# Second stage of a two-layer graph and state-space kernel: the convolution's running sum moved from SBUF to the projection's PSUM bank

## Chip, cores and metric

The kernel runs on one core of one Trainium2 chip. The metric is the device time of one execution in microseconds (us), taken as the median over several runs. The engines are TensorE (PE, matrix products; PEld is its weight load), VectorE (DVE), ScalarE (ACT), GpSimd (POOL) and SyncE (SP, which only issues transfers). Each engine works through its own list of instructions in order, and waits on semaphores for the others.

## What is computed

Two layers work on x (4096 rows of 256 numbers) and a 4096 x 4096 matrix adj. Layer 0 is a weighted neighbour sum and a Mamba-2 block, layer 1 a graph convolution with a selective scan, and a mixture of experts. The change lies in the selective scan of layer 1, whose reference is:

```python
h = jax.nn.relu(adj @ x @ gcn_w + gcn_b)
h = layer_norm(h) * ln_g + ln_b
xz = h @ w_in
xc, z = (xz[:, :D_INNER], xz[:, D_INNER:])            # D_INNER = 512
xpad = jnp.pad(xc, ((D_CONV - 1, 0), (0, 0)))         # D_CONV = 4
xconv = sum((xpad[k:k + L] * conv_w[:, k] for k in range(D_CONV))) + conv_b
u = jax.nn.silu(xconv)
dbc = u @ w_xp
dt = jax.nn.softplus(dbc[:, :DT_RANK] @ w_dt + b_dt)
B = dbc[:, DT_RANK:DT_RANK + D_STATE]                 # D_STATE = 16
C = dbc[:, DT_RANK + D_STATE:]
dA = jnp.exp(dt[:, :, None] * A[None])
dBu = dt[:, :, None] * B[:, None, :] * u[:, :, None]
def step(hst, inp):
    dAt, dBut, Ct = inp
    hst = dAt * hst + dBut
    return (hst, hst @ Ct)
_, ys = lax.scan(step, jnp.zeros((D_INNER, D_STATE), h.dtype), (dA, dBu, C))
y = ys + u * D_skip
y = y * jax.nn.silu(z)
return y @ w_out
```

## The kernel before

All data is float32. Positions are cut into 8 blocks of TB = 512, and features lie on the 128 partitions, so that D_INNER is four parts m = 0 to 3 of 128x512. The kernel has three stages. The first (to about 1110 us) is layer 0, the second (about 1110 to 2330 us) is the graph convolution and the selective scan of layer 1, the third is the mixture of experts.

In the second stage each block has 64 scan units: one for each of the 16 states n and the four parts m. A unit k is, on ACT, the exponential of dt times A into one of the PSUM banks ps4 and ps5; on POOL, the product dB of du and a broadcast row; on DVE, the recurrence itself (L1428, `scan`, h<-ps,hst,dB); and then four transposes on PE (L920) into one of the banks ps1, ps6 and ps7. The transposed result times a column of C is added to acc, on DVE (L1402), or on ACT (part) and POOL (L2199) for some (n, s), as the function `adder` says. DVE adds (`gather`) with a lag of 7 units behind its scans. The transposes of a unit on PE wait until the bank has been read, three transposes ago, and so PE cannot run more than about a unit ahead of DVE's sums, and DVE needs PE's transposes two units later.

Beside the scan of block ib run three other lists: `product_h`, PE's matmuls of adj for the blocks to come (L670, called p below); `post_b`, the output projection of the block before; and `pre_b` of the block after, which the change touches. `pre_b` normalises h (hb), then projects it part by part: b is the xc projection of part m (L856 and L858) into bank ps2, z the gate's projection (L861, L863) into bank ps3. A semaphore pair full and evac guards each bank: PE may write b of part m+1 only when b of part m has counted evac. ACT copies b to xcb (SBUF, with three columns of the block before ahead of it, the halo), and also writes tap 3 of the convolution, b times cw1 plus bias, to u (SBUF), which counts evac for the bank. DVE adds the other three taps, each one scalar_tensor_tensor (L1336) that reads xcb shifted by k and u and writes u. For each pair of parts ACT then takes tanh(u) and tanh(z's copy sz), and DVE finishes the two silu products (L1346). Last come the matmuls for dbc and dt, and the softplus of dt.

The order of the lists is fixed when the program is written. Each list is a generator that yields at slots; `beside` and `order_b` lay the 64 units of `scan` evenly over a block, the NPB slots of `pre_b` between 0.40 and 0.97 of it, and the 18 slots of `post_b` between 0.125 and 0.40. All engines follow the same list of slots, and a yield with nothing in it leaves a slot empty. `pre_load` says for each slot how much DVE work it is taken to hold; from it the table sets where PE's p matmuls go. Before the scan of block 0, `order_second` runs `pre_b(0)` beside 32 p steps alone, without POOL work; that stretch is called the opening below. So `pre_b` runs 8 times, once in the opening and 7 times beside a scan.

The lines of the prediction are: DVE L1322 and L1326 (subtraction of the mean, product with the root, hb<-hb,ps), L1336 (taps), L1346 (silu), L1355 (dt), L1402, L1428; PE L568 and L570 (mean square of the norm), L856 to L863, L670, L920; ACT L1615 (a helper, so its groups are told apart by tiles); POOL L2216 (dB) and L2199 (acc).

Of the kernel before, what the change touches and what calls it, by code (L numbers as in the profile page):

```python
# [9 lines left out]
ALU = mybir.AluOpType  # L10
ACT = mybir.ActivationFunctionType
# [111 lines left out]
def build(nc, t):  # L123
    with ExitStack() as ctx:
# [185 lines left out]

        NP, NPA, NSA, NPB, NPO = 64, 55, 62, 69, 18
        order_msg = [braid(("a", 9, 0, 1), ("b", 9, 0, 1), ("p", 16, 0, 1) if i else ("w", 4, 0.6, 1)) for i in range(NB // 2)]
# [23 lines left out]
        post_load = [1] * 8 + [0, 0] + mean_var  # L336
        pre_load = mean_var + [0, 0, 0] + ([1, 1, 0, 1, 1, 0] * 2 + [0] * 4) * 2 + [0, 2, 2, 0] + [1, 0, 1, 0, 0, 0, 0, 0, 0, 0] * 2 + [0, 0]
        beside = []
# [215 lines left out]
        def _(e):  # L554
# [291 lines left out]
            def pre_b(ib):  # L846
# [6 lines left out]
                for m in range(4):  # L853
                    b, z = preb_use(ib, 2 + 2 * m), preb_use(ib, 3 + 2 * m)
                    w.wait_ge(b.evac, b.n - 1)
                    e.matmul(b.ps[:, :], w1[:, 0, m * 128:(m + 1) * 128], hb[:, 0, :], start=True, stop=False)  # L856
                    yield
                    e.matmul(b.ps[:, :], w1[:, 1, m * 128:(m + 1) * 128], hb[:, 1, :], start=False, stop=True).then_inc(b.full, 1)  # L858
                    yield from (None, None)
                    w.wait_ge(z.evac, z.n - 1)  # L860
                    e.matmul(z.ps[:, :], w1[:, 0, 512 + m * 128:640 + m * 128], hb[:, 0, :], start=True, stop=False)  # L861
                    yield
                    e.matmul(z.ps[:, :], w1[:, 1, 512 + m * 128:640 + m * 128], hb[:, 1, :], start=False,  # L863
                             stop=True).then_inc(z.full, 1)
                    yield from (None, None)
                    if m % 2:
                        yield from (None, None, None, None)
                yield
# [196 lines left out]
        def _(e):  # L1065
# [251 lines left out]
            def pre_b(ib):  # L1317
# [11 lines left out]
                for m in range(4):  # L1329
                    b, c, at = preb_use(ib, 2 + 2 * m), u[p][:, m, :], 12 * ib + 3 * m  # L1330
                    yield from (None, None, None)
                    w.wait_ge(S("xcb"), 4 * ib + m + 1)
                    w.wait_ge(b.evac, b.n)
                    for k in range(3):
                        w.wait_ge(S("conv1"), at + k)
                        e.scalar_tensor_tensor(c, xcb[:, m, k:k + TB], col("cw1", 4 * m + k), c, ALU.mult,  # L1336
                                               ALU.add).then_inc(S("conv1"), 1)
                        yield
                    if m % 2:
                        for what in (u[p][:, m - 1:m + 1, :], sz[p][:, m - 1:m + 1, :]):  # L1340
# [262 lines left out]
        def _(e):  # L1603
# [229 lines left out]
            def pre_b(ib):  # L1833
# [8 lines left out]
                for m in range(4):  # L1842
# [7 lines left out]
                    act(xcb[:, m, 3:TB + 3], b.ps[:, :], ACT.Identity).then_inc(S("xcb"), 1)  # L1850
                    act(u[p][:, m, :], b.ps[:, :], ACT.Identity, scale=col("cw1", 4 * m + 3), bias=col("cb1", m)).then_inc(b.evac, 1)
                    yield from (None, None, None)
# [3 lines left out]
                    yield  # L1856
                    if m % 2:
                        yield
                        w.wait_ge(S("conv1"), 12 * ib + 3 * m + 3)
                        w.wait_ge(S("th1r"), n_th)  # L1860
# [6 lines left out]
                        yield  # L1867
                w.wait_ge(S("conv1"), 12 * ib + 12)
                act(xcb[:, :, 0:3], xcb[:, :, TB:TB + 3], ACT.Identity).then_inc(S("halo1"), 1)
# [422 lines left out]
```

## Time and profile before

| | us |
|---|---|
| median of 3 runs | 2549.93 (2549.86 to 2556.5) |
| the profiled execution's own time | 2553.42 |
| its span in the trace | 2551.6 |
| second stage's scans | about 1180 to 2320 |
| DVE busy over the span | 2021.9 |
| PE busy over the span | 2284.6 |

Busy time is an average over stages. Durations of neighbouring instructions in a row of the trace overlap a little: where two rows of DVE follow each other, the start of the second less the start of the first is what one costs. PE's trace shows each float32 matmul of `pre_b` and p as two records, and its rows join several; again the distance of starts counts (two records of 128x512 take 0.86 us, four of 128x256 take 0.86 us, four transposes of 128x128 0.44 us).

### The profile page before, as it was taken

The numbers are of one execution on the slowest core, as the hardware profiler recorded it, in microseconds if no ns is written. First come the engines' busy times: TensorE is split into PE (matmuls) and PEld (weight loads), VectorE is DVE, ScalarE is ACT, GpSimd is POOL, SyncE is SP. The second block draws the span as 40 slices with busy tenths as digits, with TensorE's granted clock in tenths as the row PEclk, the third lists the DMA queues.
The fourth block names the chain that finished last, engine by engine and source line by source line (L and its number), as shares of the span: only waits on it lengthen the run. The fifth ranks groups of instructions, "written<-read, shape, count | busy, mean of one in ns | idle before, by whom it ended". The sixth has DMA issues, their size and how long they took to land.

```text
span 2551.6 us, 26153 instructions
## 1 busy us (share of the span) xinstructions
PE 2284.6 (90%) x8964; PEld 1420.2 (56%) x8964; DVE 2021.9 (79%) x2224; ACT 1474.1 (58%) x2192; POOL 1198.9 (47%) x906
## 2 busy tenths in 40 slices
PE   7998999999999999988989888988998886675998
PEld 4444555545555545546666565665666563343886
DVE  5666878787877866325999999999999999997765
ACT  4676666576767553225655746565674656563444
POOL 2102231314141322305878778787887878793100
PEclk9999999999999999999989999899999998598999
DMA  5232222222222231133223232322323220112121
GB/s 214 90 98 91 66 91 87 86 75 83 88 83 86 74 124 40 51 101 124 92 83 116 75 123 76 106 92 83 116 81 118 75 91 33 42 50 79 62 67 49
DMA packets 111445, 221.15 MB, mean 87 GB/s; under 512 B 7586, under 2 KB 65186, under 8 KB 110930
## 3 DMA queue, kind: packets, MB, share of 16 engines
q1 hardware_dynamic: 107106, 204.00, 24.7%
q0 software_dynamic: 3664, 14.45, 1.5%
q8 instruction: 71, 1.16, 0.2%
q10 hardware_dynamic: 544, 1.05, 0.1%
q14 instruction: 60, 0.49, 0.1%
HBM read 199.28 MB, written 20.19 MB: 86 GB/s over the span
## 4 chain that ended last, share of the span: by engine, by line
PE 42%; DVE 24%; POOL 12%; issue 12%; ACT 9%; DMA 0%; DVEq 0%; POOLq 0%; ACTq 0%; SPq 0%
PE ps L628 9%; POOL dB L2216 7%; DVE h L1428 5%; PE ps L670 4%; DVE wgt L1106 4%; DVE wgt L1099 3%; PE ps L920 3%; DVE acc L1402 2%; PE ps L797 2%; ACT ps L1615 2%; POOL acc L2199 2%; ACT th L1615 2%; PE ps L652 2%; POOL du L2212 2%; PE ps L732 2%
## 5 line engine op out<-in xcount | busy, mean ns | idle before, releaser
L2216 POOL TENSOR_TENSOR dB<-du,bc 128x512 f32<-128x512 f32 x512 | 673.1, 1332 | 124.8 <-DVE h L1428 119.2
L1428 DVE TENSOR_TENSOR_SCAN h<-ps,hst,dB 128x512 f32<-128x512 f32 x512 | 643.4, 1271 | 48.4 <-ACT ps L1615 36.7
L628 PE MATMUL ps<-wgt,msg 128*128 128x512 f32 x1024 | 498.1, 595 | 15.1 <-DVE wgt L1106 13.6
L1615 ACT ACTIVATE ps<-dt,cols 128x512 f32<-128x512 f32 x512 | 350.9, 687 | 272.4 <-DVE h L1428 268.8
L920 PE MATMUL ps<-consts,h 128*128 128x128 f32 x2048 | 342.9, 295 | 152.3 <-DVE acc L1402 91.2
L670 PE MATMUL ps<-raw,msg 128*128 128x256 f32 x1792 | 468.9, 397 | 0.9 <-ACT hb L1615 0.9
L920 PEld LDWEIGHTS ps<-consts,h 128*128 128x128 f32 x2048 | 258.6, 150 | 335.4 <-DVE acc L1402 153.6
L670 PEld LDWEIGHTS ps<-raw,msg 128*128 128x128 f32 x1792 | 337.2, 200 | 85.8 <-issue 49.9
L628 PEld LDWEIGHTS ps<-wgt,msg 128*128 128x128 f32 x1024 | 186.6, 190 | 219.4 <-issue 191.7
L1615 ACT ACTIVATE wgt<-wgt 128x1024 f32<-128x1024 f32 x256 | 258.4, 1049 | 56.2 <-DVE wgt L1099 54.6
L2199 POOL TENSOR_TENSOR acc<-acc,part 128x512 f32<-128x512 f32 x160 | 219.4, 1371 | 87.8 <-ACT part L1615 84.1
L1402 DVE SCALAR_TENSOR_TENSOR acc<-ps,Ct,acc 128x512 f32<-128x512 f32 x305 | 220.8, 724 | 3.7 <-PE ps L920 3.6
L1099 DVE SCALAR_TENSOR_TENSOR wgt<-wgt 128x1024 f32<-128x1024 f32 x128 | 176.8, 1421 | 47.7 <-ACT wgt L1615 47.7
L1106 DVE SCALAR_TENSOR_TENSOR wgt<-raw,wgt 128x1024 f32<-128x1024 f32 x128 | 171.2, 1378 | 5.0 <-ACT wgt L1615 4.8
L1336 DVE SCALAR_TENSOR_TENSOR u<-xcb,cols,u 128x512 f32<-128x512 f32 x96 | 119.7, 1247 | 13.0 <-ACT u L1615 11.8
L1613 ACT ACT_TABLE_LOAD x78 | 100.1, 1283 | 51.5 <-DVE cc L1177 23.2
L1615 ACT ACTIVATE wgt<-raw 128x1024 f32<-128x1024 f32 x128 | 128.0, 1047 | 0.8 <-DMA raw<-in_adjT 0.6
L2142 POOL DMA_DIRECT2D tmp_x<-xb x8 | 5.5, 691 | 258.0 <-DVE xb L1260 258.0
L2111 POOL TENSOR_TENSOR E<-E,cbm 128x1024 f32<-128x1024 f32 x32 | 76.7, 2397 | 92.6 <-ACT E L1615 66.8
L1177 DVE SCALAR_TENSOR_TENSOR cc<-xbc,cols,cc 128x512 f32<-128x512 f32 x120 | 110.1, 918 | 2.9
L1615 ACT ACTIVATE part<-ps,Ct 128x512 f32<-128x512 f32 x160 | 107.3, 671 | 4.9 <-PE ps L920 4.9
L2106 POOL TENSOR_TENSOR xdec<-xdt,ecd 128x512 f32<-128x512 f32 x32 | 33.4, 1045 | 146.0 <-DVE xdt L1212 146.0
(321 smaller groups left out, 3563.4 us busy)
## 6 DMA issues: line engine op xcount, KB each, us to landing
raw<-in_adjT SPq DMA_DIRECT2D x256, 512.0 KB, 3.6
bc<-tmp_bc SPq DMA_DIRECT2D x64, 512.0 KB, 4.9
xb<-in_xT POOLq DMA_DIRECT2D x8, 512.0 KB, 4.1
tmp_x<-xb POOLq DMA_DIRECT2D x8, 512.0 KB, 3.1
x<-tmp_x SPq DMA_DIRECT2D x8, 512.0 KB, 5.4
tmp_x<-x SPq DMA_DIRECT2D x8, 512.0 KB, 4.1
raw<-tmp_xn SPq DMA_DIRECT2D x8, 512.0 KB, 4.1
tmp_xn<-x SPq DMA_DIRECT2D x7, 512.0 KB, 3.6
```

The source lines that it names most:

```text
L628: x = e.matmul(P[d][:, :], msg[:, j, d * 128:(d + 1) * 128], wgt[g % NW][:, l, :], start=j == 0, stop=j == NJ - 1)
L670: x = e.matmul(P[0][:, 256 * d:256 * d + 256], msg[:, j, d * 128:(d + 1) * 128], quarters(g)[:, l, :], start=j == 0 and d == 0, stop=j == ...
L920: i = e.transpose(b.ps[:, m * 128:(m + 1) * 128], hr[n % 3][:, m, s * 128:(s + 1) * 128], ident)
L1099: e.scalar_tensor_tensor(wgt[i % NW][:, :, :], wgt[i % NW][:, :, :], -2.0, wgt[i % NW][:, :, :], ALU.add, ALU.mult).then_inc(S("q"), 1)
L1106: e.scalar_tensor_tensor(wgt[i % NW][:, :, :], raw[i % 4][:, :, :], 1.0, wgt[i % NW][:, :, :], ALU.is_lt, ALU.mult).then_inc(S("wgt"), 1)
L1177: e.scalar_tensor_tensor(c, xbc[:, m, k:k + TB], col("cw0", 4 * m + k), c, ALU.mult, ALU.add).then_inc(S("conv"), 1)
L1336: e.scalar_tensor_tensor(c, xcb[:, m, k:k + TB], col("cw1", 4 * m + k), c, ALU.mult, ALU.add).then_inc(S("conv1"), 1)
L1402: e.scalar_tensor_tensor(acc[:, s, :], b.ps[:, :], c, acc[:, s, :], ALU.mult, ALU.add).then_inc(b.evac, 1)
L1428: e.tensor_tensor_scan(hr[n % 3][:, m, :], PS[4 + k % 2].t[:, :], dBr[k % 4][:, :], hst[:, n % 16, m:m + 1], ALU.mult, ALU.add).then_inc(S ...
L1615: return e.activation(out, in_, func, bias=bias, scale=scale)
L2199: e.tensor_tensor(acc[:, s, :], acc[:, s, :], part[HANDED[j] % 2][:, :], ALU.add).then_inc(S("summed"), 1)
L2216: e.tensor_tensor(dBr[k % 4][:, :], du[:, m, :], bcr[i % 3][:, n % 2, :], ALU.mult).then_inc(S("dB"), 1)
```

## The change

Tap 3 no longer goes to u. ACT writes it back into the projection's own bank ps2, in place, and signals a new semaphore `tap` (it first waits for its own copy to xcb). DVE's taps 0 and 1 read xcb and ps2 and write ps2; tap 2 reads xcb and ps2 and writes u in SBUF, and only it counts evac of the bank. So u is no longer an input of a tap, and the bank is held from the projection to the end of the third tap. The two tanh of ACT wait for evac where they waited for `conv1`, and `conv1` counts two taps a part where it counted three. To space the side work for this, the even parts get two more empty slots on PE, ACT and DVE, NPB goes from 69 to 73 and `pre_load` gets the zeros for them.

```diff
-        NP, NPA, NSA, NPB, NPO = 64, 55, 62, 69, 18
+        NP, NPA, NSA, NPB, NPO = 64, 55, 62, 73, 18
...
-        pre_load = mean_var + [0, 0, 0] + ([1, 1, 0, 1, 1, 0] * 2 + [0] * 4) * 2 + [0, 2, 2, 0] + [1, 0, 1, 0, 0, 0, 0, 0, 0, 0] * 2 + [0, 0]
+        pre_load = mean_var + [0, 0, 0] + ([1, 1, 0, 1, 1, 0] + [0] * 2 + [1, 1, 0, 1, 1, 0] + [0] * 4) * 2 + [0, 2, 2, 0] + [1, 0, 1, 0, 0, 0, 0, 0, 0, 0] * 2 + [0, 0]
...
# PE, pre_b, behind z of part m
-                    if m % 2:
-                        yield from (None, None, None, None)
+                    yield from [None] * (4 if m % 2 else 2)
...
# DVE, pre_b
-                    b, c, at = preb_use(ib, 2 + 2 * m), u[p][:, m, :], 12 * ib + 3 * m
+                    b, at = preb_use(ib, 2 + 2 * m), 8 * ib + 2 * m
                     yield from (None, None, None)
                     w.wait_ge(S("xcb"), 4 * ib + m + 1)
-                    w.wait_ge(b.evac, b.n)
+                    w.wait_ge(S("tap"), 4 * ib + m + 1)
                     for k in range(3):
                         w.wait_ge(S("conv1"), at + k)
-                        e.scalar_tensor_tensor(c, xcb[:, m, k:k + TB], col("cw1", 4 * m + k), c, ALU.mult,
-                                               ALU.add).then_inc(S("conv1"), 1)
+                        out, signal = (b.ps[:, :], S("conv1")) if k < 2 else (u[p][:, m, :], b.evac)
+                        e.scalar_tensor_tensor(out, xcb[:, m, k:k + TB], col("cw1", 4 * m + k), b.ps[:, :], ALU.mult,
+                                               ALU.add).then_inc(signal, 1)
                         yield
...
# ACT, pre_b
                     act(xcb[:, m, 3:TB + 3], b.ps[:, :], ACT.Identity).then_inc(S("xcb"), 1)
-                    act(u[p][:, m, :], b.ps[:, :], ACT.Identity, scale=col("cw1", 4 * m + 3), bias=col("cb1", m)).then_inc(b.evac, 1)
+                    w.wait_ge(S("xcb"), 4 * ib + m + 1)
+                    act(b.ps[:, :], b.ps[:, :], ACT.Identity, scale=col("cw1", 4 * m + 3), bias=col("cb1", m)).then_inc(S("tap"), 1)
...
-                        w.wait_ge(S("conv1"), 12 * ib + 3 * m + 3)
+                        for x in (preb_use(ib, 2 * m), b):
+                            w.wait_ge(x.evac, x.n)
```

In the following lists of instructions a row is a line, an operation and its tiles (with buffer numbers, h0 to h2 the scan's output, raw0 to raw3 adj), and the semaphores it waits for; the recurrence is printed under the name SCALAR_TENSOR_TENSOR too. Lines shift by a few behind the edit: L919 is L920 before, L1337 L1336, L1405 L1402 and L1431 L1428.

DVE, beside the scan of block 1, from the first tap of part 0 to the first tap of part 1; before:

```order
L1428 SCALAR_TENSOR_TENSOR h0<-ps5,hst,dB1 128x512 [waits dB,exp]
L1402 SCALAR_TENSOR_TENSOR acc<-ps6,Ct1,acc 128x512 [waits evac1,full6]
L1336 SCALAR_TENSOR_TENSOR u0<-xcb,cols,u0 128x512 [waits conv1,evac2,xcb]
L1336 SCALAR_TENSOR_TENSOR u0<-xcb,cols,u0 128x512 [waits conv1]
L1428 SCALAR_TENSOR_TENSOR h0<-ps4,hst,dB2 128x512 [waits dB,exp]
L1402 SCALAR_TENSOR_TENSOR acc<-ps7,Ct1,acc 128x512 [waits evac6,full7]
L1336 SCALAR_TENSOR_TENSOR u0<-xcb,cols,u0 128x512 [waits conv1]
L1428 SCALAR_TENSOR_TENSOR h0<-ps5,hst,dB3 128x512 [waits dB,exp]
L1428 SCALAR_TENSOR_TENSOR h1<-ps4,hst,dB0 128x512 [waits hst,dB,exp]
L1336 SCALAR_TENSOR_TENSOR u0<-xcb,cols,u0 128x512 [waits conv1,evac2,xcb]
```

and now:

```order
L1431 SCALAR_TENSOR_TENSOR h2<-ps5,hst,dB3 128x512 [waits dB,exp]
L1431 SCALAR_TENSOR_TENSOR h0<-ps4,hst,dB0 128x512 [waits hst,dB,exp]
L1337 SCALAR_TENSOR_TENSOR ps2<-xcb,cols,ps2 128x512 [waits tap,xcb]
L1431 SCALAR_TENSOR_TENSOR h0<-ps5,hst,dB1 128x512 [waits dB,exp]
L1405 SCALAR_TENSOR_TENSOR acc<-ps6,Ct1,acc 128x512 [waits evac1,full6]
L1337 SCALAR_TENSOR_TENSOR ps2<-xcb,cols,ps2 128x512 [waits conv1]
L1337 SCALAR_TENSOR_TENSOR u0<-xcb,cols,ps2 128x512 [waits conv1]
L1431 SCALAR_TENSOR_TENSOR h0<-ps4,hst,dB2 128x512 [waits dB,exp]
L1405 SCALAR_TENSOR_TENSOR acc<-ps7,Ct1,acc 128x512 [waits evac6,full7]
L1431 SCALAR_TENSOR_TENSOR h0<-ps5,hst,dB3 128x512 [waits dB,exp]
L1431 SCALAR_TENSOR_TENSOR h1<-ps4,hst,dB0 128x512 [waits hst,dB,exp]
L1337 SCALAR_TENSOR_TENSOR ps2<-xcb,cols,ps2 128x512 [waits tap,xcb]
```

The first tap stands one scan and one sum earlier, and three scans and one sum lie between the last tap of part 0 and the first of part 1, where two scans lay.

PE at the same place, from z of part 0 (the last rows into ps3) to the projection of part 1 into ps2; before:

```order
L861 MATMUL ps3<-hb,w1 128x512 [waits evac3]
L920 MATMUL ps1<-consts,h2 128x128 [waits scan,evac1]
L920 MATMUL ps1<-consts,h2 128x128 x3
L863 MATMUL ps3<-hb,w1 128x512
L670 MATMUL ps0<-raw2,msg 128x256 x2
L920 MATMUL ps6<-consts,h2 128x128 [waits evac6]
L920 MATMUL ps6<-consts,h2 128x128 x3
L856 MATMUL ps2<-hb,w1 128x512 [waits evac2]
L858 MATMUL ps2<-hb,w1 128x512
L920 MATMUL ps7<-consts,h2 128x128 [waits evac7]
```

and now:

```order
L863 MATMUL ps3<-hb,w1 128x512
L919 MATMUL ps1<-consts,h2 128x128 [waits scan,evac1]
L919 MATMUL ps1<-consts,h2 128x128 x3
L670 MATMUL ps0<-raw2,msg 128x256 [waits d_raw2]
L670 MATMUL ps0<-raw2,msg 128x256 x3
L919 MATMUL ps6<-consts,h2 128x128 [waits evac6]
L919 MATMUL ps6<-consts,h2 128x128 x3
L670 MATMUL ps0<-raw2,msg 128x256 x2
L856 MATMUL ps2<-hb,w1 128x512 [waits evac2]
L919 MATMUL ps7<-consts,h2 128x128 [waits evac7]
L919 MATMUL ps7<-consts,h2 128x128 x3
L858 MATMUL ps2<-hb,w1 128x512
```

Between z of part 0 and the first matmul of part 1 lay two p and one set of four transposes; now six p and two sets lie there, and a third set lies between the two matmuls of part 1.

PE at the norm of the same block (L568 and L570 read sq1 and fill ps3); before:

```order
L920 MATMUL ps1<-consts,h0 128x128 [waits evac1]
L920 MATMUL ps1<-consts,h0 128x128 x3
L568 MATMUL ps3<-sq1,consts 128x512 [waits evac3,sq1]
L920 MATMUL ps6<-consts,h0 128x128 [waits evac6]
L920 MATMUL ps6<-consts,h0 128x128 x3
L670 MATMUL ps0<-raw0,msg 128x256 x2
L570 MATMUL ps3<-sq1,consts 128x512
L920 MATMUL ps7<-consts,h1 128x128 [waits scan,evac7]
```

and now:

```order
L919 MATMUL ps1<-consts,h0 128x128 [waits evac1]
L919 MATMUL ps1<-consts,h0 128x128 x3
L568 MATMUL ps3<-sq1,consts 128x512 [waits evac3,sq1]
L570 MATMUL ps3<-sq1,consts 128x512
L919 MATMUL ps6<-consts,h0 128x128 [waits evac6]
L919 MATMUL ps6<-consts,h0 128x128 x3
L670 MATMUL ps0<-raw0,msg 128x256 x2
```

The two matmuls now stand together, without a set of transposes and a row of p between them. On DVE the product with the root (L1326 before) stands one scan and one sum closer behind the subtraction.

## Rows read from the trace of the kernel before

**Rows 1.** Page part 1: engine, busy us (share of span), instructions.

```profile
PE 2284.6 (90%) x8964; PEld 1420.2 (56%) x8964; DVE 2021.9 (79%) x2224; ACT 1474.1 (58%) x2192; POOL 1198.9 (47%) x906
```

**Rows 2.** Busy us by stretch: PE, PEld, DVE, ACT, POOL; PE clock, DMA, GB/s.

```profile
1320.00:1460.00 140.00, 124.47 (x570) 86.89 (x567) 130.06 (x129) 83.99 (x137) 108.90 (x83) 0.95 0.29 96
1390.00:1418.00 28.00, 24.28 (x109) 15.93 (x108) 27.32 (x26) 18.05 (x29) 24.26 (x17) 1.00 0.19 61
```

**Rows 3.** DVE groups, 1180 to 2320: busy us, mean ns | idle before, releaser.

```profile
L1428 DVE TENSOR_TENSOR_SCAN h<-ps,hst,dB 128x512 f32<-128x512 f32 x512 | 643.4, 1271 | 48.4 <-ACT ps L1615 36.7 <-POOL dB L2216 11.6
L1402 DVE SCALAR_TENSOR_TENSOR acc<-ps,Ct,acc 128x512 f32<-128x512 f32 x301 | 217.9, 724 | 1.2 <-PE ps L920 1.2
L1336 DVE SCALAR_TENSOR_TENSOR u<-xcb,cols,u 128x512 f32<-128x512 f32 x84 | 110.7, 1318 | 1.0
```

**Rows 4.** DVE waits, 1180 to 2320: who, for whom, us, times, longest.

```profile
DVE hb L1326 <- ACT ps L1615: 8.4, 7, 1.5
```

**Rows 5.** The taps in the opening, DVE groups 1100 to 1180.

```profile
L1336 DVE SCALAR_TENSOR_TENSOR u<-xcb,cols,u 128x512 f32<-128x512 f32 x12 | 9.0, 752 | 12.0 <-ACT u L1615 11.8
```

**Rows 6.** DVE in time: start us, us, instruction, count; taps of block 1.

```profile
1390.40 3.04 DVE L1336 SCALAR_TENSOR_TENSOR u<-xcb,cols,u 128x512 f32<-128x512 f32 x2
1393.37 1.27 DVE L1428 TENSOR_TENSOR_SCAN h<-ps,hst,dB 128x512 f32<-128x512 f32 x1
1394.56 0.72 DVE L1402 SCALAR_TENSOR_TENSOR acc<-ps,Ct,acc 128x512 f32<-128x512 f32 x1
1395.20 1.33 DVE L1336 SCALAR_TENSOR_TENSOR u<-xcb,cols,u 128x512 f32<-128x512 f32 x1
```

**Rows 7.** POOL in the same stretch, in time.

```profile
1391.16 4.82 POOL L2216 TENSOR_TENSOR dB<-du,bc 128x512 f32<-128x512 f32 x3
...
1397.81 1.27 POOL L2216 TENSOR_TENSOR dB<-du,bc 128x512 f32<-128x512 f32 x1
```

**Rows 8.** ACT groups, 1180 to 2320.

```profile
L1615 ACT ACTIVATE u<-ps,cols 128x512 f32<-128x512 f32 x28 | 21.7, 775 | 0.0
...
L1615 ACT ACTIVATE sz<-ps 128x512 f32<-128x512 f32 x28 | 16.6, 593 | 9.3 <-PE ps L863 9.3
...
L1615 ACT ACTIVATE ps<-ps 128x512 f32<-128x512 f32 x28 | 16.4, 587 | 9.7 <-PE ps L570 9.3
```

**Rows 9.** PE in time, norm and first projection of block 1.

```profile
1377.99 1.12 PE L568 MATMUL ps<-sq,consts 128*128 128x512 f32 x2
...
1380.54 1.02 PE L570 MATMUL ps<-sq,consts 128*128 128x512 f32 x2
...
1386.43 1.02 PE L856 MATMUL ps<-hb,w 128*128 128x512 f32 x2
1387.29 1.02 PE L858 MATMUL ps<-hb,w 128*128 128x512 f32 x2
1388.15 0.60 PE L920 MATMUL ps<-consts,h 128*128 128x128 f32 x4
1388.58 1.03 PE L670 MATMUL ps<-raw,msg 128*128 128x256 f32 x4
1389.45 1.02 PE L861 MATMUL ps<-hb,w 128*128 128x512 f32 x2
```

**Rows 10.** DVE in time, the product with the root.

```profile
1382.82 1.22 DVE L1326 TENSOR_TENSOR hb<-hb,ps 128x1024 f32<-128x1024 f32 x1 [1.15 <-ACT ps L1615]
```

**Rows 11.** ACT in time, opening: copy of part 2, tanh behind part 3.

```profile
1146.74 0.58 ACT L1615 ACTIVATE xcb<-ps 128x512 f32<-128x512 f32 x1
...
1155.00 1.06 ACT L1615 ACTIVATE th<-u 128x1024 f32<-128x1024 f32 x1 [0.54 <-DVE u L1336]
```

**Rows 12.** PE in time, opening: parts 2 and 3, silu-fed matmuls.

```profile
1144.20 1.02 PE L858 MATMUL ps<-hb,w 128*128 128x512 f32 x2
...
1149.37 1.02 PE L856 MATMUL ps<-hb,w 128*128 128x512 f32 x2
```

**Rows 13.** PE waits, 1180 to 2320, longest in total.

```profile
PE ps L920 <- DVE acc L1402: 91.2, 77, 3.9
```

More of the change, by code:

```diff
@@ L1329, in pre_b @@
                 for m in range(4):
-                    b, c, at = preb_use(ib, 2 + 2 * m), u[p][:, m, :], 12 * ib + 3 * m
+                    b, at = preb_use(ib, 2 + 2 * m), 8 * ib + 2 * m
                     yield from (None, None, None)
                     w.wait_ge(S("xcb"), 4 * ib + m + 1)
-                    w.wait_ge(b.evac, b.n)
+                    w.wait_ge(S("tap"), 4 * ib + m + 1)
                     for k in range(3):
                         w.wait_ge(S("conv1"), at + k)
-                        e.scalar_tensor_tensor(c, xcb[:, m, k:k + TB], col("cw1", 4 * m + k), c, ALU.mult,
-                                               ALU.add).then_inc(S("conv1"), 1)
+                        out, signal = (b.ps[:, :], S("conv1")) if k < 2 else (u[p][:, m, :], b.evac)
+                        e.scalar_tensor_tensor(out, xcb[:, m, k:k + TB], col("cw1", 4 * m + k), b.ps[:, :], ALU.mult,
+                                               ALU.add).then_inc(signal, 1)
                         yield
-                    if m % 2:
+                    if m % 2 == 0:
+                        yield from [None] * 2
+                    else:
                         for what in (u[p][:, m - 1:m + 1, :], sz[p][:, m - 1:m + 1, :]):
@@ L1856, in pre_b @@
                     yield
-                    if m % 2:
+                    if m % 2 == 0:
+                        yield from [None] * 2
+                    else:
                         yield
-                        w.wait_ge(S("conv1"), 12 * ib + 3 * m + 3)
+                        for x in (preb_use(ib, 2 * m), b):
+                            w.wait_ge(x.evac, x.n)
                         w.wait_ge(S("th1r"), n_th)
@@ L1867, in pre_b @@
                         yield
-                w.wait_ge(S("conv1"), 12 * ib + 12)
                 act(xcb[:, :, 0:3], xcb[:, :, TB:TB + 3], ACT.Identity).then_inc(S("halo1"), 1)
```

## Prediction

> **What bounds the kernel now.** I read the busy time of each engine first [rows 1], then the same by stretch [rows 2], then the groups and waits of DVE in the scans [rows 3, 4], then single instructions in time. PE has the largest share of the whole span (90%), but its share says little here, because PE's waits in the second stage are for DVE's sums: 91.2 us in 77 waits of the transposes [rows 13]. In a block of the scans (1320 to 1460) DVE is busy 130.06 us of 140, PE 124.47 and POOL 108.90; in the stretch with the taps (1390 to 1418) DVE is busy 27.32 us of 28, PE 24.28 [rows 2]. DVE waits 48.4 us for ACT and POOL before its scans in 1140 us, and before its taps 1.0 us [rows 3]. So DVE sets the pace, in the tap stretches all the more, and a microsecond that its taps lose is a microsecond of the kernel until PE or a chain takes over.
>
> What a tap costs depends on who is beside it. In the opening, with POOL idle, it takes 752 ns [rows 5]; beside the scan 1318 ns over 84 taps [rows 3]. A sum L1402 has the same size and reads one operand from PSUM, and takes 724 ns in the same stretch, 301 times over [rows 3]. The rows in time say why: two taps take 3.04 us from 1390.40 [rows 6], and POOL's three products from 1391.16 take 4.82 us, 1.6 each, where one that no tap meets takes 1.27 [rows 7]. They take turns: a tap waits for POOL's instruction in progress, and POOL's next waits for the tap. That is the price of reading both operands from SBUF.
>
> The Trainium skill ("SBUF — State Buffer", Who interferes with whom) says that a DVE instruction with two SBUF inputs contends with a GpSimd instruction that reads SBUF, and one with at most one SBUF input does not. The trace agrees, 1318 against 724 ns.
>
> **The change, part by part.** *Taps beside the scan.* Each now reads xcb from SBUF and the other operand from PSUM. I take the 724 ns of L1402: 84 x (1.318 - 0.724) = 49.9 us less DVE work. For the third tap (28 of the 84), which writes SBUF, L1402 is the same form. The first two write PSUM, and no DVE row does. The nearest are ACT's: in place in PSUM 587 ns, from PSUM to SBUF 593 [rows 8], so a PSUM output costs ACT nothing. Bounds for these 56 taps: below, the same 1% cheaper, 717 ns, which gives 0.4 us more; above, the 1.271 us of the scan [rows 3], the slowest DVE row of this size, which gives 56 x (1.271 - 0.724) = 30.6 us less gain. I take 724 ns, the nearest row in form.
> A rule speaks against the change: by the Trainium skill ("Perfetto Trace Analysis", Optimizing Scalar/DVE Operations) a DVE access costs about 60 ns on SBUF and 125 on PSUM. By it, as an estimate, the 84 taps would lose 65 ns each, 5.5 us in all. L1402 with a PSUM operand is not above the quiet 752 ns, so the trace does not show it.
>
> *Taps in the opening.* 12 x (752 - 724) ns, 0.3 us, nothing.
>
> *ACT.* The write to u (775 ns) becomes one to ps2 [rows 8], at the same price. New is the wait for its own copy to xcb: at present the second starts 0.49 us after the first though the first lasts 0.6; I put 0.15 us on each of 28, 4 us of ACT in all. ACT is busy 84 us of 140 [rows 2], so it counts only in the chains below.
>
> *POOL.* It gets back what the taps made it wait, some 0.3 us for each product that met one. DVE waited for dB only 11.6 us in all [rows 3], so I count nothing.
>
> *The longer hold.* This is the price. Before, PE could project part m+1 as soon as ACT had read part m. Now it waits for the last tap. The slots place the first matmul of part m+1 about one scan unit behind that tap on PE's list, and PE is tied to DVE by the transposes anyway. By starts, a scan costs 1.19 us and a sum 0.64 [rows 6], a projection matmul 0.86, four transposes 0.43 and two p 0.87 [rows 9]. For parts 0 to 1, counted from the end of the last tap: PE's first matmul to 0.95; the transposes behind it wait for DVE's next sum, at 1.83, to 2.27; the second matmul to 3.1; ACT's copy and write back 0.5 + 0.15 + 0.7 with 0.1 us for each signal, to about 4.65. DVE meanwhile has three scans and one sum, 3 x 1.19 + 0.64 = 4.2 us, and so waits 0.45 us. Parts 2 to 3 have the same distance: 0.45 us. Parts 1 to 2 have the silu products between and wait for nothing.
> The first tap of part 0 also has less room, as PE's two matmuls now have two p and a set of transposes between them. Before, the two stood together from 1386.43 to 1388.15 [rows 9], and the tap came at 1390.40 without a wait [rows 6]: 2.25 us, of which ACT's two writes need 1.4, so 0.85 were to spare. The chain is now longer by 0.87 + 0.43 on PE and 0.15 on ACT, 1.45 us: 0.6 us of it is not covered.
> In the norm the root's product stands one scan and one sum closer (1.83 us), where DVE waited 1.15 us already in this block [rows 10] and 8.4 us in seven [rows 4]. But L570 now follows L568 at once instead of 2.55 us later (1377.99 and 1380.54, [rows 9]), so that the root comes 1.7 us sooner. Net 0.3 us.
> Before the tanh of the second pair DVE has one scan less cover: 0.2 us. Together 0.45 + 0.45 + 0.6 + 0.3 + 0.2 = 2.0 us a block, 14 us in seven blocks.
>
> *The opening.* Part 2 is projected by 1144.20 + 0.86 = 1145.06 [rows 12], ACT's copy comes at 1146.74 [rows 11], so the three taps end at about 1150.5. PE has five pieces of 0.86 us (p, z) before part 3 and is there at 1149.4: it waits 1.1 us. A further p pair stands between part 3's matmuls, 0.9 us. The tanh at 1155.00 [rows 11] comes 2 us later, and the start of the scans with it: +2 us.
>
> **Sum.** -49.9 + 14 + 2 = -34 us. Of the profiled execution's 2553.4 us that leaves 2519.5; the median of the three runs is 3.5 us lower, so I predict 2516.
>
> **The rivals.**
> *A, the full gain.* The waits are covered after all, since a wait at one tap fills the queues and spares the next wait (DVE's 36.7 us for ACT [rows 3] may shrink too): 2550 - 50 = 2500. For it: the table gives one unit of distance; against: three scans and a sum are just the length of the chain.
> *B, PE becomes the bound in the tap stretch.* PE has 16 projection matmuls (13.8 us), about 32 p (13.8) and 17 sets of transposes (7.3) in the 17 units from the first projection to the last: 34.9 us. DVE there needs 36 us after the change and 43 before. If PE needs idle time at the share of now (24.28 busy of 28, [rows 2]), the stretch takes 40.2 us, and a block gains 3 us instead of 5: 7 x 3 - 2 = 19 us, 2530.
> *C, PSUM outputs are slow on DVE.* At 1.271 us for 56 taps: -49.9 + 30.6 + 16 = -3, so 2547, no change that can be told.
> *D, slower: the handover between parts falls out of step.* PE waits for the last tap with scan transposes queued behind it; DVE's next sum waits for those, and only after it come DVE's next scans and taps. Then the chain of two matmuls and two ACT writes, 3.3 us, is not covered but added. With 3 handovers in each of 7 blocks it costs 69 us, and 2550 - 50 + 69 + 2 = 2571. It decides against the change once a handover costs DVE more than 50/21 = 2.4 us, that is, lasts over 6.6 us where 4.2 are covered. Against it: in DVE's list the taps come behind the sum for which PE's transposes wait, and PE reaches the wait about a unit after the tap.
> *E, the taps are bound by something else than POOL* (the kernel does not do what it says, 1318 ns stay): 2550 + 16 = 2566. The 752 ns of the opening [rows 5] speak against it.
>
> **How the numbers follow.** Forecast 0.45, A 0.19, B 0.18, C 0.09, D 0.05, E 0.04. The range from 2498 to 2538 holds the forecast, A and B with some PSUM cost on each. A measurement of this kernel tells about 0.3% (8 us) from no change. Faster by more: forecast, A and B, and a little of C, 0.84. Within: most of C, 0.09. Slower: D, E and rest, 0.07.
>
> **What would show it.** The taps' groups: about 724 ns for both outputs, POOL's products near 1270 ns. DVE's idle before the first taps of parts 1 and 3 of some 0.4 us each, released by ACT, where it was nothing; before the root's product a little over 1.15 us. PE's waits at L856 for the tap short, under 0.5 us beside the scan, about 1 us once in the opening. DVE's busy time falls by 50 us; the span falls by less, and the difference stands as idle before taps. I am wrong if the taps that write PSUM read over 0.85 us, if DVE's scans and sums begin to wait for PE by more than 10 us in all (B), or if the first taps wait over 2 us each (D).

## The result

The changed kernel takes 2512.04 us (median of 4 runs, 2511.06 to 2513.26), against 2553.12 us (4 runs, 2549.86 to 2556.5) for the kernel before on the same chip. The ratio is 0.9839, with a 95% interval of 0.9821 to 0.9858, so it is 41 us (1.6%) faster. The forecast was 2516 us. The span of the profiled execution fell from 2551.6 to 2509.5 us, by 42.1 us.

The groups of DVE in the scans of the changed kernel answer to [rows 3] (busy us, mean ns | idle before, releaser):

```profile
L1431 DVE TENSOR_TENSOR_SCAN h<-ps,hst,dB 128x512 f32<-128x512 f32 x512 | 643.1, 1271 | 39.0 <-ACT ps L1618 27.4 <-POOL dB L2222 11.6
L1405 DVE SCALAR_TENSOR_TENSOR acc<-ps,Ct,acc 128x512 f32<-128x512 f32 x301 | 218.1, 725 | 1.8 <-PE ps L919 1.7
L1337 DVE SCALAR_TENSOR_TENSOR ps<-xcb,cols,ps 128x512 f32<-128x512 f32 x56 | 41.9, 748 | 19.1 <-ACT ps L1618 19.1
...
L1349 DVE SCALAR_TENSOR_TENSOR sz<-th,sz 128x1024 f32<-128x1024 f32 x14 | 21.6, 1539 | 0.0
L1337 DVE SCALAR_TENSOR_TENSOR u<-xcb,cols,ps 128x512 f32<-128x512 f32 x28 | 20.9, 748 | 1.0
...
L1349 DVE SCALAR_TENSOR_TENSOR u<-th,u 128x1024 f32<-128x1024 f32 x14 | 17.2, 1225 | 4.4 <-ACT th L1618 4.4
L1358 DVE SCALAR_TENSOR_TENSOR dt<-dt,th 128x1024 f32<-128x1024 f32 x14 | 16.9, 1207 | 0.0
...
L1325 DVE TENSOR_TENSOR hb<-hb,ps 128x1024 f32<-128x1024 f32 x7 | 8.5, 1221 | 11.3 <-ACT ps L1618 11.3
```

The taps take 748 ns in both forms, where they took 1318, and the form that writes PSUM costs what the form that writes SBUF does. The 84 taps now need 41.9 + 20.9 = 62.8 us instead of 110.7. But DVE now waits 20.1 us before them, where it waited 1.0. Two groups of the kernel before belong beside the others:

```profile
L1346 DVE SCALAR_TENSOR_TENSOR u<-th,u 128x1024 f32<-128x1024 f32 x14 | 22.6, 1613 | 4.0 <-ACT th L1615 4.0
...
L1346 DVE SCALAR_TENSOR_TENSOR sz<-th,sz 128x1024 f32<-128x1024 f32 x14 | 17.9, 1280 | 0.0
L1355 DVE SCALAR_TENSOR_TENSOR dt<-dt,th 128x1024 f32<-128x1024 f32 x14 | 17.5, 1250 | 4.0 <-ACT th L1615 4.0
```

DVE's time between the first scan and the last, by group (busy and idle before it):

| us | before | after | difference |
|---|---|---|---|
| taps, busy | 110.7 | 62.8 | -47.9 |
| taps, wait | 1.0 | 20.1 | +19.1 |
| root's product, wait | 8.4 | 11.3 | +2.9 |
| scans, wait for ACT | 36.7 | 27.4 | -9.3 |
| dt, wait and busy | 21.5 | 16.9 | -4.6 |
| silu, wait and busy | 44.5 | 43.2 | -1.3 |
| sum | | | -41.1 |

The first scan starts at 1181.14 us instead of 1180.08, the last at 2277.7 instead of 2317.5, so the scans shrank by 40.9 us. Behind the last scan 231.8 us are left where 234.1 were. That is TensorE's clock: the work is the same and the waits of PE behind the scans are alike, but the granted clock of the first 50 us there (a mean of its two levels, 1.2 and 2.4 GHz, as a share of the upper) was 0.80 before and 0.86 after. The same two pairs of matmul records there took 2.08 and 1.65 us before, and 1.12 and 1.02 after. Whether the change has a part in the clock is not shown. Both rows are of the view by stretches: from and to, length, the busy time of PE, PEld, DVE, ACT and POOL with their counts, then PE's granted clock, the DMA share and GB/s. The kernel before:

```profile
2330.00:2380.00 50.00, 32.67 (x109) 21.66 (x108) 34.70 (x63) 17.02 (x28) 4.11 (x2) 0.80 0.34 120
```

The changed kernel, in the same place of the program:

```profile
2289.00:2339.00 50.00, 32.68 (x117) 21.90 (x116) 36.11 (x66) 17.36 (x28) 4.15 (x2) 0.86 0.36 127
```

POOL in the tap stretch of block 1, in time, shows what answers to [rows 7]: no product takes over 1.28 us.

```profile
1385.63 1.28 POOL L2205 TENSOR_TENSOR acc<-acc,part 128x512 f32<-128x512 f32 x1 [1.35 <-ACT part L1618]
1386.86 2.50 POOL L2222 TENSOR_TENSOR dB<-du,bc 128x512 f32<-128x512 f32 x2
...
1391.07 1.27 POOL L2205 TENSOR_TENSOR acc<-acc,part 128x512 f32<-128x512 f32 x1
```

DVE at the handover from part 0 to part 1 of block 1 in the changed kernel, in time (start, length, instruction, idle before it and its releaser):

```profile
1387.72 0.75 DVE L1337 SCALAR_TENSOR_TENSOR u<-xcb,cols,ps 128x512 f32<-128x512 f32 x1
...
1393.40 0.76 DVE L1337 SCALAR_TENSOR_TENSOR ps<-xcb,cols,ps 128x512 f32<-128x512 f32 x1 [0.73 <-ACT ps L1618]
```

PE in the same place of the changed kernel, in time:

```profile
1389.13 1.02 PE L856 MATMUL ps<-hb,w 128*128 128x512 f32 x2
1390.36 0.66 PE L919 MATMUL ps<-consts,h 128*128 128x128 f32 x4 [0.21 <-DVE acc L1405]
1390.86 1.02 PE L858 MATMUL ps<-hb,w 128*128 128x512 f32 x2
```

The last tap of part 0 ends at 1388.39, and PE comes to the projection of part 1 (L856) at 1389.13 by its own list, not held by the bank. Then a set of transposes waits 0.21 us for DVE's sum, and only at 1390.86 does the second matmul (L858) start. ACT's copy and write follow, and DVE has waited 0.73 us when the next tap starts at 1393.40.

### The profile page after: what moved, and what is told of

Its sections match the earlier page's. It is cut to its first block, busy times and chain, and to the rows that moved or that the text cites. A ratio compares the mean times of both kernels' runs of the same rounds, so it can differ in the third digit from the quotient of the medians.

```text
span 2509.5 us, 26161 instructions
## 1 busy us (share of the span) xinstructions
PE 2276.5 (91%) x8964; PEld 1413.7 (56%) x8964; DVE 1971.0 (79%) x2224; ACT 1475.5 (59%) x2192; POOL 1186.5 (47%) x906
## 3 DMA queue, kind: packets, MB, share of 16 engines
q8 instruction: 71, 1.16, 0.2%
q10 hardware_dynamic: 544, 1.05, 0.1%
## 4 chain that ended last, share of the span: by engine, by line
PE 41%; DVE 24%; issue 13%; POOL 12%; ACT 9%; DMA 1%; DVEq 0%; SPq 0%; POOLq 0%; ACTq 0%
PE ps L628 9%; POOL dB L2222 8%; DVE h L1431 5%; DVE wgt L1105 4%; PE ps L670 3%; DVE wgt L1098 3%; PE ps L919 2%; DVE acc L1405 2%; PE ps L797 2%; POOL acc L2205 2%; ACT th L1618 2%; ACT ps L1618 2%; PE ps L903 2%; PE ps L652 2%; PE ps L732 2%
## 5 line engine op out<-in xcount | busy, mean ns | idle before, releaser
L2222 POOL TENSOR_TENSOR dB<-du,bc 128x512 f32<-128x512 f32 x512 | 663.7, 1314 | 102.6 <-DVE h L1431 98.4
L1431 DVE TENSOR_TENSOR_SCAN h<-ps,hst,dB 128x512 f32<-128x512 f32 x512 | 643.1, 1271 | 39.0 <-ACT ps L1618 27.4
L670 PE MATMUL ps<-raw,msg 128*128 128x256 f32 x1792 | 456.8, 392 | 0.9 <-ACT hb L1618 0.9
L919 PE MATMUL ps<-consts,h 128*128 128x128 f32 x2048 | 339.0, 292 | 114.6 <-DVE acc L1405 58.2
L919 PEld LDWEIGHTS ps<-consts,h 128*128 128x128 f32 x2048 | 254.8, 149 | 296.6 <-DVE acc L1405 126.9
L1405 DVE SCALAR_TENSOR_TENSOR acc<-ps,Ct,acc 128x512 f32<-128x512 f32 x305 | 221.0, 725 | 4.2 <-PE ps L919 4.0
L1618 ACT ACTIVATE g<-ps,b 128x512 f32<-128x512 f32 x64 | 43.2, 687 | 81.9 <-PE ps L1002 74.3
```

What stands on the lines that cost most here:

```text
L670: x = e.matmul(P[0][:, 256 * d:256 * d + 256], msg[:, j, d * 128:(d + 1) * 128], quarters(g)[:, l, :], start=j == 0 and d == 0, stop=j == ...
L919: i = e.transpose(b.ps[:, m * 128:(m + 1) * 128], hr[n % 3][:, m, s * 128:(s + 1) * 128], ident)
L1405: e.scalar_tensor_tensor(acc[:, s, :], b.ps[:, :], c, acc[:, s, :], ALU.mult, ALU.add).then_inc(b.evac, 1)
L1431: e.tensor_tensor_scan(hr[n % 3][:, m, :], PS[4 + k % 2].t[:, :], dBr[k % 4][:, :], hst[:, n % 16, m:m + 1], ALU.mult, ALU.add).then_inc(S ...
L1618: return e.activation(out, in_, func, bias=bias, scale=scale)
L2222: e.tensor_tensor(dBr[k % 4][:, :], du[:, m, :], bcr[i % 3][:, n % 2, :], ALU.mult).then_inc(S("dB"), 1)
```

## The experiments

### Which part of the change does it: the spacing or the sum in PSUM

**Spacing alone.** The kernel before with 73 slots and the empty slots, the sum in SBUF:

```diff
-        NP, NPA, NSA, NPB, NPO = 64, 55, 62, 69, 18
+        NP, NPA, NSA, NPB, NPO = 64, 55, 62, 73, 18
...
-                    if m % 2:
-                        yield from (None, None, None, None)
+                    yield from [None] * (4 if m % 2 else 2)
```

(with the zeros in `pre_load`, and two empty slots behind the even parts on DVE and ACT too).

> The kernel before with only the spacing of the change: 73 slots, two empty slots behind the even parts on PE, ACT and DVE, the running sum in SBUF as before. Theory (the gain is the taps' own time): taps stay at about 1318 ns beside the scan, 2553 us within 8 us; a few us less are possible if the shorter waits of the scans for ACT (27.4 us after, 36.7 before) come from the spacing. Rival (the spacing brings the gain, by spreading PE's and DVE's side work): 2530 us or less.

Measured: 2561.44 us against 2555.13, ratio 1.0025 (1.0016 to 1.0035), a loss of 6 us. DVE's groups there:

```profile
L1429 DVE TENSOR_TENSOR_SCAN h<-ps,hst,dB 128x512 f32<-128x512 f32 x474 | 596.5, 1272 | 40.3 <-ACT ps L1616 28.7 <-POOL dB L2219 11.6
...
L1335 DVE SCALAR_TENSOR_TENSOR u<-xcb,cols,u 128x512 f32<-128x512 f32 x84 | 117.9, 1404 | 14.5 <-ACT xcb L1616 10.6 <-issue 3.0
...
L1356 DVE SCALAR_TENSOR_TENSOR dt<-dt,th 128x1024 f32<-128x1024 f32 x14 | 16.9, 1208 | 0.0
```

The taps are slower still, 1404 ns, and DVE waits 14.5 us before them, though no bank is held. The scans' wait for ACT is down to 28.7 us and dt's wait is gone: these two savings of the changed kernel come from the spacing. They do not pay for the waits and the slower taps. (The view ends at 2270, 38 scans short; the waits of the scans are the same to the last scan.)

**The sum in PSUM without the spacing.** The changed kernel with 69 slots and without the empty slots:

```diff
-        NP, NPA, NSA, NPB, NPO = 64, 55, 62, 73, 18
+        NP, NPA, NSA, NPB, NPO = 64, 55, 62, 69, 18
...
-                    yield from [None] * (4 if m % 2 else 2)
+                    if m % 2:
+                        yield from (None, None, None, None)
```

> The changed kernel with the old 69 slots and no empty slots behind the even parts: the sum in PSUM alone. Theory (the hold is paid in the handover from the last tap to the next part's first): taps stay at 748 ns, but the first taps of parts 1 and 3 have two scans to cover the chain where they have three and a sum; 1.8 us more wait at 14 places, about 25 us, 2530 to 2540 us. Rival (the hold is harmless, PE comes late enough anyway): 2505 to 2516 us.

Measured: 2546.65 us, ratio 0.9965 (0.9951 to 0.998). It is 8 us faster than the kernel before and 35 us slower than the changed one, somewhat above the range expected. Who waited for whom there, with the total in us, the number of times and the longest; first DVE:

```profile
DVE ps L1338 <- ACT ps L1617: 38.6, 14, 5.4
```

And PE of the same kernel:

```profile
PE ps L856 <- DVE u L1338: 33.3, 14, 3.1
```

PE stands at the bank for 33.3 us at 14 places, and DVE waits 38.6 us for ACT before the taps. This is the price of the hold when nothing is placed for it. The sum in PSUM and the spacing are worth little each alone, -8 and +6 us, and -41 together.

### Whose wait is it: the bank's, or that of two matmuls that stand apart

In the changed kernel a set of transposes stands between the two projection matmuls of a part, in parts 0 and 3 with a row of p as well; in part 1 of block 1 that set waits for DVE (the 0.21 us above). The next edit removes the slot between them:

```diff
                     e.matmul(b.ps[:, :], w1[:, 0, m * 128:(m + 1) * 128], hb[:, 0, :], start=True, stop=False)
-                    yield
                     e.matmul(b.ps[:, :], w1[:, 1, m * 128:(m + 1) * 128], hb[:, 1, :], start=False, stop=True).then_inc(b.full, 1)
-                    yield from (None, None)
+                    yield from (None, None, None)
```

**In the changed kernel.**

> The changed kernel with the two projection matmuls of each part in one slot of PE's list, so that no transposes or p stand between them; number of slots as in the changed kernel. Theory (DVE's 19.1 us before the first taps are the chain from the last tap through PE's set of transposes, which waits for DVE's sum): the second matmul ends at 1.8 us instead of 3.1 us behind the last tap, the waits of parts 1 and 3 vanish and part 0's falls from 1.05 to about 0.2 us; 10 to 17 us less, 2495 to 2503 us. Rival (those waits stand for a PE that is the bound in the tap stretch): the waits move to DVE's sums or scans, 2508 to 2514 us.

Measured: 2495.55 us, ratio 0.9767 (0.975 to 0.9783), 16.5 us less than the changed kernel. DVE's waits between the scans in this kernel:

```profile
DVE h L1430 <- ACT ps L1617: 28.2, 30, 2.1
...
DVE ps L1336 <- ACT ps L1617: 4.1, 9, 1.2
```

DVE's wait for ACT before the taps fell from 19.1 us in 21 places to 4.1 in 9. Its wait for PE's transposes before the sums stayed (1.7 us to the last scan in both kernels), and so did the scans' for ACT (28.2 us, 27.4 in the changed kernel).

**With the sum in SBUF and the spacing.**

> The kernel before with the spacing and with the two projection matmuls of each part together; the sum in SBUF. Theory (standing together only shortens the chain behind the hold): the same as spacing alone, 2561 us within 6. Rival (it speeds PE or ACT up in general, the 16.5 us it gave the changed kernel have nothing to do with the hold): 2545 us.

Measured: 2543.84 us, ratio 0.9957 (0.994 to 0.9973). The theory failed: the same edit gains 17.6 us over spacing alone (2561.44), where no bank is held until the last tap. DVE's wait before the taps fell from 14.5 to 2.8 us:

```profile
L1334 DVE SCALAR_TENSOR_TENSOR u<-xcb,cols,u 128x512 f32<-128x512 f32 x84 | 120.7, 1437 | 2.8 <-ACT xcb L1615 1.8
```

So most of the wait that I had put down to the hold is the chain from PE's first matmul to the tap, stretched by the transposes between the two matmuls. The spacing shifted the slots so that this happens for part 0 and part 1, too.

**In the kernel before.**

> The kernel before with only the two projection matmuls of each part together. Theory (their standing apart costs only where DVE's taps come up against the chain from the projection, and in the kernel before they wait 1.0 us in all): no change, 2548 to 2558 us. Rival (it is a gain of about 17 us in any layout, as it was behind the spacing with either form of the sum): 2538 us.

Measured: 2554.62 us against 2554.36, ratio 1.0 (0.9991 to 1.001). Where DVE does not wait before its taps, the edit is worth nothing. The theory held here: the edit gains 16 to 18 us with the spacing in either form of the sum, where DVE waits before its taps, and nothing here.

**With the sum in PSUM and no spacing.**

> The sum in PSUM with the old 69 slots (no spacing), and the two projection matmuls of each part together. In the sum-in-PSUM run without spacing DVE waited 39.1 us before its taps, at 14 places, two of them in each block, and PE 33.3 us at the projection for the last tap; in that layout parts 0 and 1 had their matmuls together already, parts 2 and 3 apart. Theory (without spacing the hold itself is the wait: PE stands at the bank right behind the last tap's slot): only the parts with matmuls apart gain, about 7 x 2 us, 2528 to 2536 us, and PE's wait at the projection stays near 33 us. Rival (also there the waits come from the matmuls standing apart): the waits fall below 10 us and the time to 2505 us or less.

Measured: 2530.94 us, ratio 0.9904 (0.9887 to 0.992), 16 us less than without the edit. So the gain needs no spacing either, only a wait of DVE before its taps. That wait fell from 38.6 to 27.4 us: before part 3, whose matmuls stood apart, from 4.1 or 4.2 us to between 2.1 and 3.0 in the five middle blocks, while before part 1, whose matmuls stood together already, 1.19 us stayed. PE's wait at the bank in this kernel:

```profile
PE ps L856 <- DVE u L1337: 32.4, 14, 3.3
```

PE's wait at the bank stayed (32.4 us), as expected. So without the spacing the hold costs, and the spacing takes that away (5.9 us with it, in the changed kernel with the matmuls together).

The medians beside each other, in us (they come from several chips, on which the kernel before has medians of 2553 to 2556, so that a difference between two of them is good to about 3 us):

| | sum in SBUF | sum in PSUM |
|---|---|---|
| old slots, matmuls as they were | 2555 | 2546.65 |
| old slots, together | 2554.62 | 2530.94 |
| spacing, matmuls as they were | 2561.44 | 2512.04 |
| spacing, together | 2543.84 | 2495.55 |

With the spacing, the sum in PSUM is worth 49 us in one row and 48 in the other. Without it 8 and 24.

### Why a tap with two SBUF inputs is slow

**POOL reads nothing.** Both products of POOL become fills with zeros:

```diff
-                e.tensor_tensor(acc[:, s, :], acc[:, s, :], part[HANDED[j] % 2][:, :], ALU.add).then_inc(S("summed"), 1)
+                e.memset(acc[:, s, :], 0.0).then_inc(S("summed"), 1)
...
-                e.tensor_tensor(dBr[k % 4][:, :], du[:, m, :], bcr[i % 3][:, n % 2, :], ALU.mult).then_inc(S("dB"), 1)
+                e.memset(dBr[k % 4][:, :], 0.0).then_inc(S("dB"), 1)
```

> The kernel before with POOL's two scan products replaced by a fill with zeros of the same tiles (no product du x bc, no sum acc + part: this part of the computation is left out), so that POOL reads no SBUF there. Theory (a tap waits because POOL reads SBUF): the taps L1336 beside the scan take about 750 ns as in the opening, min to max within 0.1 us. Rival (they wait for something else in the scans, such as transfers or ACT's writes): 1300 ns.

Measured, in one run: 2481.97 us. The taps beside the scan:

```profile
L1336 DVE SCALAR_TENSOR_TENSOR u<-xcb,cols,u 128x512 f32<-128x512 f32 x84 | 62.4, 743 | 2.4 <-ACT xcb L1615 1.4
```

84 taps in the SBUF form take 743 ns (724 to 753 over all 96), with POOL still writing 665 tiles of the same size in that stretch. The fills do meet taps: in block 1 two of them, at 1384.50 and 1384.96, lie within two taps that together took 1.51 us from 1383.88. So a tap waits for POOL's reading of SBUF, and not for its writing, for transfers or for ACT, which went on as before. The time of this kernel says less, because POOL itself became faster (526 ns a fill, where a product took 1332), and part of the work is gone.

**One tap of each form.** ACT writes tap 3 to u; the three taps of DVE are then

```diff
-                        out, signal = (b.ps[:, :], S("conv1")) if k < 2 else (u[p][:, m, :], b.evac)
+                        part_, bank = u[p][:, m, :], b.ps[:, :]
+                        out, old, signal = ((bank, part_, S("conv1")), (part_, bank, S("conv1")), (part_, part_, b.evac))[k]
```

> The changed kernel and its spacing, but with ACT's tap 3 in SBUF (u), tap 0 from xcb and u (both SBUF) to PSUM, tap 1 from xcb and PSUM to u, tap 2 from xcb and u to u. Theory (two SBUF inputs make a tap wait for POOL, where it writes does not matter): the first and third form 1300 ns, the second 748 ns; 56 slow taps at 0.57 us more are 32 us, 2540 to 2548 us. Rival (the SBUF output is what meets POOL): the first form 750 ns, the other two 1300 ns, the same time. Rival (reading PSUM alone is enough to be fast only if the output is PSUM too): the second form is slow.

Measured: 2520.88 us, ratio 0.9862 (0.9846 to 0.9879). The three groups of taps in this kernel:

```profile
L1338 DVE SCALAR_TENSOR_TENSOR ps<-xcb,cols,u 128x512 f32<-128x512 f32 x28 | 24.1, 861 | 20.2 <-ACT u L1619 20.2
L1338 DVE SCALAR_TENSOR_TENSOR u<-xcb,cols,u 128x512 f32<-128x512 f32 x28 | 23.7, 846 | 1.0
...
L1338 DVE SCALAR_TENSOR_TENSOR u<-xcb,cols,ps 128x512 f32<-128x512 f32 x28 | 20.6, 735 | 0.0
```

The order of the forms is that of the theory: both forms with two SBUF inputs meet POOL, whether they write PSUM (861 ns) or SBUF (846), and the one with a PSUM input does not (735). The size is not: they lose about 0.11 us each and not 0.57, and the kernel lost 9 us and not 32. Part by part, the first tap took 0.76 us in the 14 places behind a scan, and behind a sum 0.77 in 7 places and 1.16 in 7; in the kernel before, two taps back to back took 1.2 to 1.5 us each on average (a row of 3.04 us for two, [rows 6]), and the second of such a pair 1.64 or 1.65 wherever the trace shows it by itself. My reading is that a tap loses what is left of POOL's product when it comes, and that a second one right behind it finds the next product ahead of it; the rows fit this, but no run tests it alone.

**The sum ahead of the scan.** In the kernel before, DVE's sum of each unit moved ahead of its scan, so that no tap stands behind a sum:

```diff
+                    j = k - LAG
+                    if j > 0 and j % 64 == 0:
+                        gates(j // 64 - 1)
+                    if j >= 0:
+                        gather(j)
                     if k < 64 * NB:
...
-                    j = k - LAG
-                    if j > 0 and j % 64 == 0:
-                        gates(j // 64 - 1)
-                    if j >= 0:
-                        gather(j)
                     yield
```

> The kernel before with DVE's sum of each unit ahead of its scan instead of behind it, so that every tap stands behind a scan or another tap, and none behind a sum. In the one-tap-of-each-form run, taps with two SBUF inputs took 0.76 us behind a scan and 0.77 to 1.16 behind a sum, and the changed kernel's gain would then depend on POOL's phase. Theory (a tap waits only for what is left of POOL's product, and POOL starts one when a scan ends): single taps 0.76 to 0.85 us, the second of a pair 1.2 to 1.6, the mean 1.0 to 1.1 us, so 20 us less than before if the sums are hidden as before, 2525 to 2540 us. Rival (every tap meets POOL at a random point): the mean stays at 1.3 us and the time at 2550 or above.

Measured: 2546.34 us, ratio 0.9982 with an interval of 0.996 to 1.0003, so a gain is not shown. Five of the six runs lie between 2544.66 and 2547.03, below all nine of the kernel before (2550.1 to 2555.89), and the sixth took 2561.19 at a mean granted clock of 0.946, where the others had 0.961 to 0.963. A gain of some 9 us is likely, then, and it is well short of the 2525 to 2540 us expected. DVE's groups in the scans of this kernel:

```profile
L1336 DVE SCALAR_TENSOR_TENSOR u<-xcb,cols,u 128x512 f32<-128x512 f32 x84 | 99.7, 1187 | 1.0
...
L1346 DVE SCALAR_TENSOR_TENSOR sz<-th,sz 128x1024 f32<-128x1024 f32 x14 | 25.1, 1791 | 0.0
...
L1355 DVE SCALAR_TENSOR_TENSOR dt<-dt,th 128x1024 f32<-128x1024 f32 x14 | 21.6, 1543 | 8.5 <-ACT th L1615 8.5
```

The taps' mean fell to 1187 ns, 11 us less in all, half of what I expected: single taps behind a scan took 0.72 to 0.79 us in 14 places, but 1.12 to 1.14 in the other 14. The other instructions with two SBUF inputs came to stand worse: the silu product sz<-th,sz went to 1791 ns from 1280, dt to 1543 from 1250. The place beside POOL matters, but moving one thing moves all, and which phase decides stays open. What does not stay open is that an input from PSUM removes the meeting in every place: in the kernel with one tap of each form all 28 taps of that form took 0.73 or 0.74 us, and the 84 of the changed kernel took 0.74 to 0.76.

### A faster version

**Matmuls together, and the root's product one slot later.** On DVE in `pre_b`, six empty slots ahead of the product with the root and four behind it, where five and five stood.

> The changed kernel with the two matmuls together, and on DVE the norm's product with the root one slot later (behind one scan and one sum more), the number of slots unchanged. It waits 1.6 us a block for the root now. Theory: that wait goes (11.3 us), but the chain from there to part 0's first tap has one scan and a sum less cover, about 1.0 us of 1.6 comes back there: 0 to 5 us less than with the matmuls together, 2490 to 2496 us. Rival (that wait was all cover for others): 2496 to 2500 us.

Measured: 2491.16 us (2490.67 to 2492.59), ratio 0.9754 (0.9738 to 0.977), the fastest of the kernels that compute everything. DVE's waits between the scans in this kernel:

```profile
DVE h L1430 <- ACT ps L1617: 30.8, 39, 2.1
DVE ps L1336 <- ACT ps L1617: 6.7, 14, 0.6
```

The wait for the root falls from 11.3 to 1.1 us; the taps wait 6.7 us instead of 4.1, and the scans for ACT 30.8 instead of 28.2 and for POOL 10.7 instead of 11.6, from the first scan to the last. The gain of 4.4 us over the kernel with the matmuls together lies in the range expected. The times of the two kernels do not overlap (2494.67 to 2497.42 there), but they are from two chips and the intervals of their ratios do overlap, so the gain is likely and not shown.

## Why the prediction was right, and where it was not

**The taps.** 49.9 us forecast, 47.9 measured. The price of 724 ns was 24 ns low: the taps take 748, close to their 752 in the quiet opening ([rows 5]), so that this row would have been the better choice. What the 24 ns are is open; a DVE instruction with a scalar from cols and one input in PSUM (L1411 before) takes 734. The open bound, the write to PSUM, costs nothing (rival C falls). The reason, POOL's reading, is shown by the fill experiment; rival E falls. The Trainium skill ("SBUF — State Buffer", Who interferes with whom) draws the same line, at a GpSimd instruction that reads SBUF and not at one that only writes it, and the 743 ns beside the fills agree. Its charge of 125 ns for an access to PSUM against 60 to SBUF ("Perfetto Trace Analysis", Optimizing Scalar/DVE Operations) is not seen: 748 ns for either output, and 752 with SBUF alone.

**ACT and POOL.** ACT's write to ps2 takes 751 ns (775 before) and starts 0.63 us behind the copy instead of 0.49, as forecast (0.15 us). POOL's gain brought nothing, as forecast: DVE waited 11.6 us for it before and after.

**The longer hold.** Here a step failed. I forecast 1.5 us a block of waits before taps (0.6, 0.45 and 0.45), and 2.7 came on average (1.05, 0.73 and 0.68 in block 1). The places and the releaser were right, and the transposes between the matmuls were in my chain, but I called the sum of it the price of the hold. The runs say otherwise. With the sum in SBUF the spacing alone makes DVE wait 14.5 us; with the matmuls together 5.1 us are left in the changed kernel, and 2.8 in SBUF. By these differences the hold itself costs 2 to 6 us of DVE's waits with the spacing, and the rest is the spacing's own doing. The hold shows at one handover: PE waits 0.79 us for the last tap before it projects part 3, once in each block, where I had put under 0.5 us. The slots that were put in for the longer hold moved the two matmuls of parts 0 and 1 apart.

**Norm, silu, opening.** The root's product waits 2.9 us more in seven blocks (2.1 forecast), the silu 0.4 (1.4). The 2.1 did not follow from its own terms: 1.83 us less cover and a root 1.7 us sooner leave 0.1 us a block and not 0.3, and 0.4 came. The opening costs 1.06 us and not 2: PE's wait for the last tap of part 2 was 1.26 us (1.1 forecast), but the norm's two matmuls together, which I counted in the blocks, help in the opening too, where the root's product starts at 1125.20 instead of 1126.64.

**What was missing.** The sum ended at -34 us and -42.1 came. The difference is what I did not look for: more room between the pieces of `pre_b` also shortens waits. The scans wait 9.3 us less for ACT and dt 4.0 us less, which the spacing alone shows as well (28.7 us and none). That makes up for the waits before the taps, 19.1 us where 10.5 were forecast. The last 2.3 us are TensorE's clock behind the scans. So the size was met partly by errors that cancel. The base helped too: I subtracted from 2550 us, the median of three runs, and the median of four is 2553. From there the sum gives 2519, 7 us above the measured time and not 4.

**The rivals.** A (2500) was 12 us off, the forecast 4. The scans' wait for ACT did shrink, but not for A's reason, that a wait at a tap spares the next wait: with the matmuls together the taps hardly wait (4.1 us) and the scans still wait 28.2 us for ACT, in SBUF 2.8 and 25.9. The smaller wait comes with the spacing. B falls: DVE waited for PE's transposes 1.8 + 2.3 us, where 1.2 + 2.2 stood. D did not come, but without the spacing it begins: PE held for 33 us, DVE for 39.

## What to carry to other kernels

An instruction of DVE that reads both inputs from SBUF while POOL reads SBUF costs up to twice its time (here up to 1.65 us where it takes 0.75 undisturbed); if one of the inputs has just come out of PSUM, leaving it there saves that, at the price of a bank. Before paying for the bank with empty slots, look at what the slots pull apart: the two matmuls that fill one PSUM bank should stand together where an engine waits for the second. And an edit that frees the pacing engine should be costed with the waits elsewhere, since some fall and some rise.

## What the runs showed of the hardware

- DVE writes PSUM at the speed at which it writes SBUF: 748 ns for either output, 128x512 float32, two tensor inputs (one of them in PSUM) and a scalar.
- The delay beside POOL is no fixed charge. For the same form, 0.72 to 1.65 us were seen in one kernel (the sum ahead of the scan), in steps that repeat from block to block, and taps in a row fare worst. It slows POOL as well: 1.6 us a product in the tap stretch ([rows 7]), 1.27 without.
- POOL's fill of a tile (526 ns) does not disturb a DVE instruction with two SBUF inputs: 724 to 753 ns over 96 taps in the fill kernel.
